# Linear attention and expert block on one core: TensorE issues its base matmuls ahead of the mask transposes and of the second LoRA matmul

## What is computed

```python
logits = jnp.einsum('bsd,ed->bse', x, Wg) + bg
scores = jax.nn.softmax(logits, axis=-1)
topv, topi = jax.lax.top_k(scores, TOP_K)
w = jnp.sum(jax.nn.one_hot(topi, E, dtype=x.dtype) * topv[..., None], axis=-2)
base = jnp.einsum('bsd,fd->bsf', x, Wi)
lora_low = jnp.einsum('bsd,erd->bser', x, A)
lora = jnp.einsum('bser,efr->bsef', lora_low, B)
h = jax.nn.relu(base[:, :, None, :] + lora)
expert_out = jnp.einsum('bsef,df->bsed', h, Wo)
out = jnp.einsum('bse,bsed->bsd', w, expert_out)
```

## Time and profile before

| what | value |
|---|---|
| median of 3 executions | 795.62 us (795.56 to 798.09) |
| the profiled execution, its own time | 795.56 us |
| its span, first to last instruction | 793.3 us |
| PE busy | 747.9 us, 94% of the span |
| PE weight loads busy | 607.1 us |
| DVE busy | 531.9 us, 67% |
| ACT busy | 427.4 us, 54% |
| POOL busy | 62.8 us, 8% |
| mean granted clock of PE | 0.986 |

### The profile page before, as it was taken

One profiled execution on the slowest core, in us unless ns is written; L12 is line 12 of the kernel. 1 busy time (PEld: TensorE's weight loads), 2 busy tenths in 40 slices (PEclk: granted clock), 3 DMA queues, 4 the chain that ended last, 5 costly groups with the idle time before them and its releaser, 6 DMA issues.

```text
span 793.3 us, 16997 instructions
## 1 busy us (share of the span) xinstructions
PE 747.9 (94%) x6138; PEld 607.1 (77%) x6138; DVE 531.9 (67%) x1264; ACT 427.4 (54%) x776; POOL 62.8 (8%) x72
## 2 busy tenths in 40 slices
PE   3889999999999999999999999999999999998696
PEld 3678768887698868887698877987688876986476
DVE  4366776676766776676766767767767767666365
ACT  3376636664547645665466745565356645563232
POOL 1260110001000010001000010000100010000100
PEclk9999999999999999999999999999999999999689
DMA  8750173104801074102811056001731039000000
GB/s 283 200 138 2 54 198 75 53 0 126 196 1 53 26 197 100 53 0 79 209 36 53 8 151 165 26 26 53 188 83 53 0 108 211 5 28 28 0 1 28
DMA packets 42804, 65.36 MB, mean 82 GB/s; under 512 B 5000, under 2 KB 19104, under 8 KB 42656
## 3 DMA queue, kind: packets, MB, share of 16 engines
q1 hardware_dynamic: 42784, 65.09, 30.4%
HBM read 39.91 MB, written 25.17 MB: 82 GB/s over the span
## 4 chain that ended last, share of the span: by engine, by line
PE 81%; DVE 9%; ACT 3%; issue 2%; DMA 2%; POOL 1%; DVEq 0%; SPq 0%; ACTq 0%; POOLq 0%
PE pa L531 11%; PE prod L544 7%; PE ring L510 5%; PE ring L388 5%; PE pa L388 5%; PE pa L389 5%; PE pa L390 5%; PE ring L390 4%; PE ring L389 4%; PE ring L564 4%; PE pa L646 4%; PE ring L515 3%; PE ring L674 2%; PE ring L571 2%; DVE am_phk L1123 2%
## 5 line engine op out<-in xcount | busy, mean ns | idle before, releaser
L531 PE MATMUL pa<-phq,phkT 128*128 128x128 f32 x768 | 101.2, 275 | 0.0
L1123 DVE TENSOR_TENSOR am_phk<-pa,const 128x512 f32<-128x512 f32 x112 | 77.0, 689 | 35.6 <-PE pa L531 34.6
L531 PEld LDWEIGHTS pa<-phq,phkT 128*128 128x128 f32 x768 | 95.4, 192 | 2.1
L1291 DVE SCALAR_TENSOR_TENSOR am_phk<-ring,am_phk 128x512 f32<-128x512 f32 x64 | 44.2, 691 | 49.3 <-PE ring L727 49.1
L388 PE MATMUL pa<-wo_r,qk_r 128*128 128x256 f32 x256 | 72.2, 282 | 0.6 <-DVE qk_l L1296 0.6
L389 PE MATMUL pa<-wo_r,qk_l 128*128 128x256 f32 x256 | 72.1, 282 | 0.0
L390 PE MATMUL pa<-wo_l,qk_r 128*128 128x256 f32 x256 | 72.0, 281 | 0.0
L510 PE MATMUL ring<-xq,omega_x 100*128 100x512 f32 x196 | 70.4, 440 | 1.4 <-DVE lora_w L1116 1.4
L870 ACT ACTIVATE phq<-ring 128x512 f32<-128x512 f32 x82 | 49.3, 602 | 36.1 <-PE ring L510 35.0
L940 ACT ACTIVATE qk_r<-phq 128x512 fp32r<-128x512 f32 x64 | 40.5, 633 | 51.0 <-DVE phq L1300 51.0
L870 ACT ACTIVATE phkT<-ring 128x512 f32<-128x512 f32 x98 | 58.3, 595 | 12.9 <-PE ring L510 12.6
(11 more groups left out here) (205 smaller groups left out, 1630.0 us busy)
## 6 DMA issues: line engine op xcount, KB each, us to landing
xq<-qk_parts SPq DMA_DIRECT2D x48, 512.0 KB
qk_parts<-qk_r SPq DMA_DIRECT2D x32, 256.0 KB, 4.8
qk_parts<-qk_l SPq DMA_DIRECT2D x32, 256.0 KB, 5.2
tok<-in_L_attn_x SPq DMA_DIRECT2D x8, 512.0 KB, 3.6
xr<-in_L_attn_x SPq DMA_DIRECT2D x8, 512.0 KB, 3.4
out_x<-tg SPq DMA_DIRECT2D x16, 256.0 KB, 2.2
norm_parts<-norm_r SPq DMA_DIRECT2D x16, 128.0 KB, 2.5
norm_parts<-norm_l SPq DMA_DIRECT2D x16, 128.0 KB, 3.0
```

The lines of the kernel that those rows point to most:

```text
L531: mm = pe.matmul(score_bank(q, a)[:, tt], phkT[:, q % 2, a, tt], query(q)[:, a, tt], start=True, stop=True)
L1123: dve.tensor_tensor(am[:, 2 * (q % 2) + a, :].rearrange("p (c t) -> p c t", c=NT), score_bank(q, a)[:].rearrange("p (c t) -> p c t", c=NT) ...
L1291: dve.scalar_tensor_tensor(r2[:, f % 2, :], z_bank[f % 4][:], 0.0, rho, ALU.max, ALU.mult).then_inc(r2_done.sem, 1)
```

## The change

Two moves in the program of PE; no other engine's program changes, and no instruction is added or left out.

```diff
@@ ffn_head
                 base(n, 2)
                 wait(pe, low_high, n, 1)
-                base(n, 3, [0])
-                masks(n)
-                base(n, 3, [1])
+                base(n, 3)
@@ experts
                     if f == 0:
                         wait(pe, rt, n, 22)
                         ratio(n)
+                    if 4 <= f + 2 < FT:
+                        base(n, f + 2)
                     if 1 <= f <= FT:
                         if f == 1:
                             wait(pe, low_masked, n, 2)
...
                         for _ in range(AHEAD.get(f, 0)):
                             features(n + 1, tile // TILES, [tile % TILES])
                             tile += 1
-                    if 4 <= f + 2 < FT:
-                        base(n, f + 2)
                     if f >= 3:
@@ after_attend
                 ffn_head(n, front_next)
+                masks(n)
                 experts(n, front_next)
```

## The result

| | before | after |
|---|---|---|
| median | 796.24 us (794.82 to 798.09, 6 executions) | 803.68 us (803.04 to 805.09, 6 executions) |
| span of the profiled execution | 793.3 us | 801.0 us |
| mean granted clock of PE in it | 0.986 | 0.986 |

The ratio after to before is 1.0092, with a 95% interval of 1.0074 to 1.0109: slower by 7.4 us between the medians and by 7.7 us between the two profiled spans. The forecast was 803.7 us. That it hits the median to a few hundredths is partly chance: the working was some 0.5 us too high (8.15 for 7.7 between the spans), and the median of before over six executions is 0.6 us higher than over the three that it started from. Of the executions of the kernel before that the experiments are compared with, one took 929.69 us at a mean granted clock of 0.751 and is left out.

A forecast was written before the change was run, and what follows sets the result against it. PE was taken to bound the kernel, busy 94% of the span with 81% of the chain. Seven blocks at 0.95 us plus 1.5 in the last gave 8.15 on 795.56, so 803.7 us, range 801.0 to 805.5.

The forecast's parts named there:

- Part 1: Masks behind all of base(3): low1 moves with the transposes, PE stands still, z1(0) starts 0.70 us later per block.
- the cover: The half of base(3) behind the masks covered just low1's time before z1(0), with nothing left over.
- Part 2: base(f+2) ahead of z2(f-1): base(4) waits for r2(0), base(5) for r2(1); 0.24 us per block in the loop.
- the distance from DVE's end to PE's resumption: Unit price for PE resuming after DVE: taken as 0.09 us, with 0.05 and 0.12 as the ends for the range.
- The restart of 0.10: After a wait, PE's first matmul costs 0.10 us more, as its weight load is no longer covered.
- The last block: No features, so only z1(3) lies between z2(1) and base(5): 1.5 us later in all, bounds 1.4 to 1.65.
- The sum: Whole kernel: 7 x 0.95 + 1.5 = 8.15 us on the profiled execution's 795.56, which is 803.7.
- swallowed further on: Rival: a later stage's wait absorbs the delay; half swallowed 799.6 us, nearly all 796.5; chances 0.06 and 0.04.
- the cover that I put at 0.8 us: At Wo(3), behind z2(4): time between g_l(3)'s end and Wo(3) shrinks from 2.3 to 0.8 us and holds.
- The page's rule: Weight loads pulled ahead would make base(5)'s restart free, the sum 0.8 us lower and the time 802.9; the row favoured more.

The follow-up runs named there:

- the move alone: The kernel before with all of base(3) ahead of the mask transposes and the loop of experts unchanged; ratio 1.0066, 5.3 us slower.
- one matmul: The kernel before with one matmul of base(3)'s second half ahead of the mask transposes instead of all three; ratio 1.0016, 1.3 us slower.
- the run with base(4) alone: The kernel before with base(4) ahead of z2(1) in round 2 only, base(5) to base(7) left in place; expected 0.6 us faster, measured ratio 1.0021.
- the second of the faster kernels: The kernel before with one feature, then base(4), ahead of z2(1) in round 2, the other feature behind; ratio 0.9957, 3.4 us faster.

## Why the prediction was right

*Part 1.* Expected at 0.70 a block with the cause in low1; the period of the move alone rose by 0.69, and with one matmul by 0.25. The claim that the cover was used up exactly was read from one row, the weight load of z1(0) 0.12 after low1's end, and it held. In the last block I took 0.67; there, masks to z1(0) takes 770.57 - 769.13 = 1.44 where it was 1.57, so the 0.70 comes down to 0.57. The spare time there was 0.13, not some hundredths. It did not show in the block's sum, since z1(0) to z1(4) lost 0.89 there (8.43 against 7.54) where 0.83 was reckoned.

*Part 2.* Expected at 0.24 in the loop; it was 0.18. base(4) was held by r2(0), and base(5) by r2(1), as worked out. The term that was too large is the distance from DVE's end to PE's resumption: I took 0.09, between ACT's 0.05 and the 0.12 of low1, and it is 0.05 (214.34 to 214.39) and 0.06 (217.01 to 217.07), which is ACT's distance. The 0.12 of low1 belongs to z1(0) in the loop and should not have been carried over to r2: after the change, where z1(0) surely waits, its weight load again starts 0.11 behind low1's end (211.78), while in the last block it starts 0.05 behind it (770.52). Its loads in the second and in the last block:

```profile
211.89 0.19 PEld L715 LDWEIGHTS ring<-norm_r,lora_w 96*128 96x128 f32 x1 [0.75 <-issue]
...
770.57 0.19 PEld L715 LDWEIGHTS ring<-norm_r,lora_w 96*128 96x128 f32 x1 [0.66 <-DVE norm_r L1282]
```

What holds it in the loop was not traced. r2(1) starts 0.42 behind its z2, not 0.44. The restart of 0.10 held: base(4) and what follows take 215.90 - 214.39 = 1.51.

*The last block.* Expected at 1.5 in all. PE's timeline after:

```profile
769.13 1.03 PE L696 MATMUL pa<-const,mk 128*96 128x128 f32 x8
770.57 0.50 PE L715 MATMUL ring<-norm_r,lora_w 96*128 96x512 f32 x1 [0.41 <-DVE norm_r L1282]
...
775.85 0.50 PE L388 MATMUL ring<-h_r,wi_r 128*128 128x512 f32 x1 [0.56 <-DVE am_phk L1290]
...
779.00 0.40 PE L715 MATMUL ring<-norm_r,lora_w 96*128 96x512 f32 x1
```

From the masks to z1(4) it takes 9.87 where it took 9.11; with 0.70 for the later masks this is 1.46. base(5) waits there (0.56 of idle) as there is nothing between z2(1) and it.

*The sum* with the measured terms is 8 x 0.70 + 7 x 0.18 + 0.76 = 7.6, against 8.15 forecast and 7.7 between the spans. In the loop nothing was swallowed further on: the period rose by what the stage lost. Outside it two differences that no term stands for happen to cancel in part. z1(0) of the first block came only 0.29 later (119.25 to 119.54) where 0.70 was due, and the wait for a DMA ahead of it was 0.3 shorter (3.7 for 4.0); and z1(0) of the seventh block to that of the last took 96.64 where it had taken 95.68, 0.2 more than the terms give. Both stretches hold times of low clock and differ from run to run (see the last section). In the loop no Wo waited for g_l: in the second block g_l(3) ended at 227.10 and Wo(3) started at 227.97, so the cover that I put at 0.8 us was 0.9.

*What the prediction did not see* is the wait of the feature of round 3 for its exponential. It made no difference here, since base(5)'s wait stands in its place, but it turned the expected sign of the run with base(4) alone.

*The page's rule.* The Trainium skill says that weight loads are pulled ahead of matmuls in flight ("TensorE: Matmul & The Clock Gate", "Step-by-step: what each phase is for"). I had reckoned that by this rule base(5) would start without a restart. The load of base(5) stood idle for 0.52 and then started with its matmul at 217.07, and the next matmul came at 217.41, 0.34 later where 0.233 is the pace. In these rows a load runs ahead where nothing waits, and waits where its matmul waits. The row decides, and the 0.10 was due.

## What to carry to other kernels

A wait is covered only from the moment at which the filler itself is ready. base(4) looked like filler for z2(1)'s wait for relu(1), but its own bank was freed only 0.17 us before that wait ended, and z2(1) and the features behind it became 1.2 to 1.4 us later; a feature, which was ready early enough, gave 0.23 us a block. Before moving work ahead of a short instruction, ask who waits for that instruction and for those queued with it, on every engine; and where an operand arrives with nothing to spare, as low1 did, what stands between its producer and its consumer is cover and costs its full length when it goes.

## What was not expected of the hardware

The executions of one kernel spread over some 3.6 us (795.1 to 798.8 for the kernel before in the experiments), more than several of the effects here, and the time goes with the mean granted clock of the execution: 795.1 to 795.8 where it is 0.986, 797.9 to 798.8 where it is 0.979. The traces show where. The loop repeats to hundredths in every kernel. Two stretches do not. The time up to z1(0) of the first block is 119.25 in the trace of before and up to 121.3 in others whose edits stand behind it; the granted clock from 40 to 60 us is 0.91 in the former and 0.76 in the latter. And the last block has no front of a next block beside it, PE stands still there for up to 3.8 us at a time, and its granted clock falls to 1.2 GHz for stretches that differ from run to run. The windows of the run with base(4) alone, and of the second of the faster kernels (columns: stretch, length, busy time of PE, PEld, DVE, ACT and POOL, granted clock, DMA share, GB/s):

```profile
735.00:745.00 10.00, 6.67 (x48) 5.05 (x49) 2.23 (x7) 1.19 (x2) 2.35 (x1) 0.50 0.00 0
745.00:755.00 10.00, 6.19 (x20) 4.87 (x20) 4.31 (x15) 1.09 (x2) 1.38 (x2) 0.67 0.00 0
755.00:765.00 10.00, 9.28 (x26) 5.34 (x25) 4.57 (x16) 3.15 (x6) 0.00 (x0) 0.63 0.01 2
```

```profile
735.00:745.00 10.00, 5.47 (x28) 4.23 (x28) 4.53 (x17) 1.09 (x2) 2.68 (x2) 0.99 0.00 0
745.00:755.00 10.00, 8.10 (x18) 4.64 (x18) 3.52 (x6) 4.10 (x7) 1.04 (x2) 0.50 0.01 2
755.00:765.00 10.00, 9.71 (x47) 6.95 (x46) 7.39 (x30) 2.91 (x6) 0.00 (x0) 1.00 0.00 0
```

In the first the clock is low for most of 30 us, in the second for 10. The distance from z1(0) of the seventh block to that of the eighth was 95.7 before, 97.7 in the first of these and 92.6 in the second; the edits account for 0.1 more and 0.2 less of it, by the experts of the seventh block. I did not test what sets the rest. For effects of this size the period of the loop, read from one trace, tells more than the times do: it separated 0.07 us a block, where the blocks of one trace repeat to 0.03.
